# A fused attention and expert kernel: factor loads ahead of the values' stage, quantiser levels respread, five of them in the projection

## The chip, the core and the metric

The kernel runs on one core of one Trainium2 chip. The metric is device time in microseconds (us), median of three runs. Everything is fp32; matrix products are made of float32r products of high and low parts, three for each product.

The engines by the names of the profile: PE is TensorE (PEld its weight loads), DVE VectorE, ACT ScalarE, POOL GpSimd, SP SyncE, which here issues nearly all DMAs.

## What is computed

```python
x = x + attn(cond(x, itok, cond_weights), Wq, bq, Wk, bk, Wv, bv, Wo, bo, gq, gk)
x = x + ffn(cond2(x, weight, scale_log, codebook, lora_A, lora_B), A, B, Wr, br)

# cond:  W = weights[condition]; einsum('bct,bcd->bdt', x, W)      64 x 32 tokens of 512
# attn:  q, k, v = h @ W + b; RMS norm of q and k over all 4096; 32 heads of 128;
#        softmax(q k^T / sqrt(128)) v over the 32 tokens of a batch; @ Wo + bo
# cond2: a 512 x 512 weight is quantised to a 64-entry codebook
lora_delta = lora_B @ lora_A * (LORA_ALPHA / LORA_RANK)
wg = (weight + lora_delta).reshape(O, I // GROUP, GROUP)
normalized = wg / scale
idx = jnp.searchsorted(thresholds, normalized, side='left')
quantized = cb[idx]
w = jax.lax.stop_gradient(quantized - normalized) + normalized
w_eff = (w * scale).reshape(O, I) + lora_delta
return x @ w_eff.T
# ffn:   router softmax over 8 experts, low-rank A then B, weighted sum
```

## The kernel before

The 2048 tokens are 16 tiles of 128. The kernel has four parts, one after the other on TensorE.

**Mixing** forms the conditioned tokens.

**Queries and keys**: 64 steps `s`, two for each of 32 heads. Each is a block product in Strassen form: seven products `p1` to `p7` of six matmuls of 512 columns. ScalarE copies sums out of the banks (`keep_a1`, `keep_a2`, `keep_a3`), VectorE finishes the four output blocks (`block_11`, `block_12`, `block_22`; ScalarE makes the fourth), GpSimd adds squares for the norms.

**Values**: 32 more steps, `s` = 64 to 95, numbered `u` = 0 to 31, of the same seven products with the raw weights `wv` as the moving operand. The weights come in eight quads; ScalarE makes the high parts (`split_v`), and `low_v` the low parts: on VectorE at first, on GpSimd from quad 1 on, but for `low_v(1, 1)` and `low_v(2, 1)`, which VectorE does in step `u` = 0. Each output block goes from `v_out` to `v_spill` in DRAM by a store of SyncE (`store_v`), and the next block of that kind waits for the store. Two steps in, `lora(1)` multiplies the LoRA factors `la` and `lbt`.

**Projection**: 64 head pairs, in a loop over even `b`, 16 for each of four chunks `c` of tokens. A step of the loop is `pv(b)`, `pv(b + 1)` (attention weights times values), `project_out(b - 1)`, `project_out(b)`. ScalarE writes the high part of what `pv` gives (`out_hi`), VectorE the low part (`out_lo`, line 1951), which `project_out` and the pair after next wait for. VectorE also does the softmax's `shift` and `invert`, each every second step, and the transposes of the weights; GpSimd scales and normalises them and makes the low parts of the output weights (`low_o`). In between come `low_product`, which joins the effective weights with the experts' matrices, and for each chunk the residual, the router and the experts.

The **quantiser** is VectorE's filler work. A weight half of 128x1024 is built up from 63 levels: `level(half, t)` compares with a threshold, scales by the codebook step (line 1724) and adds to the sum (line 1725). After them come `straight_through` (lines 1728, 1729) and `effective` (lines 1734, 1735). Half 0 runs in the queries' stage, half 1 in the values' stage, placed by `levels_v`: one level between `block_11(s + 1)` and `block_12(s)`, the others after `block_12(s)`. Every engine takes its instructions in the order written here, with semaphores between the engines; nothing is reordered by a scheduler.

Half 1 lives in `accr`: `qv` in columns 0 to 1023, `qf` in 1024 to 2047, `update` in 2048 to 3071. `qm`, the scratch of a level, is columns 3072 to 4095 of `qreg`, where the factors `la` and `lbt` are loaded too. `xr`, two buffers of 2048 columns, holds the residual tiles of the chunks.

Of the kernel before, what the change touches and what calls it, by code (L numbers as in the profile page):

```python
# [8 lines left out]
ALU = mybir.AluOpType  # L9
# [3 lines left out]
P = 128  # L13
B, C, D = 64, 32, 512
KI = D // P
# [16 lines left out]
RANK = 64  # L32
# [23 lines left out]
V_ORDER = (0, 4, 1, 5, 2, 6, 3, 7)  # L56
B_LOW = 4
STEPS = NCH * NP
# [26 lines left out]
def levels_v(s):  # L85

    u = s - N_QK
    if u < 5 or u >= 28:
        return {28: 1}.get(u, 0)
    return 3 if u % 2 == 0 or (u % 4 == 1 and u > 5) else 2  # L90

# [19 lines left out]
def build(nc, x_nat, x_tr, cond_w, cond_idx, codebook, wqk, wv_in, wo_in, vecs, bo, w2, scale_log,  # L111
# [4 lines left out]
    with ExitStack() as ctx:  # L116
# [111 lines left out]
        wo_raw = [qk[:, 2048:3072]] + [spare[:, 1024 * (p % 2 == 0):1024 * (p % 2 == 0) + 1024] for p in range(1, NP)]  # L228
        xr = [accr[:, k:k + 2048].rearrange("p (i n) -> p i n", i=KI) for k in (0, 2048)]
        awr_sb = small[:, 0:KI * LR].rearrange("p (i n) -> p i n", i=KI)  # L230
# [200 lines left out]
        def _(sp):  # L431
# [50 lines left out]
            for s in range(1, N_QK):  # L482
                if s % 2 == 1 and (s + 3) // 2 < H:
                    load_raw((s + 3) // 2)
                if s == N_QK - 3:
                    load_v_raw(0, 0)
                if s == N_QK - 2:
                    load_v_raw(0, 1)
                if s % 2 == 0:
                    sp.wait_ge(kept, s // 2)  # L490
                    sp.dma_start(spill[s // 2 - 1], stage).then_inc(spilled, 16)
# [4 lines left out]
            load_v_raw(1, 1)  # L496
            sp.wait_ge(w_eff_done, 1)
            for rows in (slice(0, RANK), slice(RANK, P)):
                sp.dma_start(la[rows], lora_a).then_inc(ld_lora[1], 16)
                sp.dma_start(lbt[rows], lora_bt).then_inc(ld_lora[1], 16)  # L500

# [85 lines left out]
            def load_res(c):  # L587
                if c <= 1:
                    sp.wait_ge(low_raw, 2)
                else:  # L590
                    sp.wait_ge(stored, 16 * KI * (c - 1))
                sp.dma_start(xr[c % 2], x_tr[:, :, c * CH:(c + 1) * CH]).then_inc(ld_res[c % 2], 16)
# [5 lines left out]
            for b in range(2, STEPS, 2):  # L598
                c, p = b // NP, b % NP
                if b == 2:  # L600
                    for k in (11, 12, 21, 22):
                        sp.wait_ge(v_stored[k], 16 * N_V)
                if c >= 1 and p in (10, 12):
                    store_out(c - 1, p - 10)
                    store_out(c - 1, p - 9)
                if b + 2 < STEPS:
                    load_v(b + 2)
                    load_v(b + 3)
                if b + 2 < NP:
                    load_wo(b + 2)  # L610
                    load_wo(b + 3)
                if b % 4 == 0 and b // 4 + 2 < NG:
                    load_scores(b // 4 + 2)
                if b == 2 * B_LOW:
                    sp.wait_ge(low_raw, 2)
                    load_res(0)
                    sp.dma_start(b_sb, bmat).then_inc(ld_ffn, 16)
                if c == 1 and p == 2:
                    load_res(1)
                if c >= 1 and p == 14 and c + 1 < NCH:  # L620
                    load_res(c + 1)
# [458 lines left out]
        def _(act):  # L1080
# [322 lines left out]
            for b in range(2, STEPS, 2):  # L1403
# [7 lines left out]
                if b == B_LOW:  # L1411
                    low_keep(0)
                    low_keep(1)
                if b == 12:
                    act.wait_ge(ld_ffn, 48)
                    act.activation(b_part[0], b_sb, ACT.Copy).then_inc(b_hi, 1)
# [39 lines left out]
        def _(pool):  # L1456
# [129 lines left out]
            for b in range(2, STEPS, 2):  # L1586
# [6 lines left out]
                if b % 4 == 0 and b // 4 + 1 < NG:  # L1593
                    normalise(b // 4 + 1)
                if b == 16:
                    pool.wait_ge(b_hi, 1)
                    pool.tensor_tensor(b_part[1], b_sb, b_part[0].bitcast(F32), ALU.subtract).then_inc(b_lo, 1)

        @block.vector
        def _(dve):  # L1600
            chained = [0]

            def link(ins):
                chained[0] += 1
                ins.then_inc(chain, 1)
                dve.wait_ge(chain, chained[0])
# [119 lines left out]

            def straight_through(half):
                link(dve.tensor_tensor(qf[half], qf[half], qv[half], ALU.subtract))
                link(dve.tensor_tensor(qf[half], qf[half], qv[half], ALU.add))

# [227 lines left out]
            for s in range(N_QK, N_ST):  # L1958
                u = s - N_QK
                block_22(s)  # L1960
                if s + 1 < N_ST:
                    block_11(s + 1)
                if u == 1:
                    variances()
# [21 lines left out]
                block_12(s)  # L1986
                if u == 0:
                    low_v(1, 1)
                    low_v(2, 1)
                if u == 4:  # L1990
# [5 lines left out]
                if u == 28:  # L1996
                    shift(0)
                if u == 29:
                    straight_through(1)
                    effective(1)  # L2000
                if u == 30:
# [3 lines left out]
            invert(1)  # L2005
            assert taken == NCODE - 1
            def residual(c, outputs=range(KI)):
# [41 lines left out]
            for b in range(2, STEPS, 2):  # L2049
# [26 lines left out]
                if b % 4 == 0 and b // 4 + 1 < NG:  # L2076
                    invert(b // 4 + 1)
            residual(NCH - 1)

# [89 lines left out]
```

## Time and profile before

| | us |
|---|---|
| median of 3 runs | 1458.38 |
| the three runs | 1458.02, 1458.38, 1461.37 |
| the profiled execution | 1457.52 |
| its span, first to last instruction | 1455.7 |
| TensorE busy | 1447.5 (99%) |
| VectorE busy | 1082.1 (74%) |
| GpSimd busy | 750.7 (52%) |
| ScalarE busy | 726.5 (50%) |
| mean granted TensorE clock | 0.999 of full speed |

Times in the profile are from the span's start. The values' stage is from about 681 to 1006, the projection from there to the end. A row of a timeline gives start, duration, engine, line, operation, written and read tiles, shapes and count, and in square brackets the idle time of the engine before it with what ended it.

### The profile page before, as it was taken

To read this page: it belongs to the slowest core of one execution; us is meant where nothing else is said; L and a number is where in the kernel's file an instruction comes from. 1 tells how busy PE (TensorE), PEld (TensorE's weight loads), DVE (VectorE), ACT (ScalarE), POOL (GpSimd) and SP (SyncE) were. 2 spreads that over 40 slices of the span, in tenths; PEclk is the share of its full clock that TensorE was granted. 3 is DMA by queue.
4 is the path that set the end of the run, shared out by engine and by line. 5 is a ranking of instruction groups with operands and counts; after the bars stand their busy time and mean duration, and the time that the engine had idled before them with its cause. 6 is when DMAs were issued, how large, how long until landed. Compare 5 with 4: busy or idle time off the path is not lost.

```text
span 1455.7 us, 34717 instructions
## 1 busy us (share of the span) xinstructions
PE 1447.5 (99%) x14507; PEld 1201.8 (83%) x14507; DVE 1082.1 (74%) x1507; ACT 726.5 (50%) x1331; POOL 750.7 (52%) x530
## 2 busy tenths in 40 slices
PE   9999999999999999999999999999999999999999
PEld 8788888888888888888788888889888888888887
DVE  8788868687786877874469989988567667677663
ACT  7766676766766666766333333334442222222221
POOL 7668777787777777776345555514452112112100
PEclk9999999999999999999999999999999999999999
DMA  4211011110111111111443344447563334244230
GB/s 152 66 45 45 31 38 44 45 45 23 45 45 45 31 37 45 45 44 52 132 154 128 133 135 145 138 139 260 160 214 130 100 120 132 77 141 133 74 117 30
DMA packets 106989, 135.13 MB, mean 93 GB/s; under 512 B 6224, under 2 KB 89424, under 8 KB 106320
## 3 DMA queue, kind: packets, MB, share of 16 engines
q1 hardware_dynamic: 105968, 132.49, 27.6%
q8 instruction: 114, 1.87, 0.6%
q10 hardware_dynamic: 864, 0.42, 0.1%
q14 instruction: 43, 0.35, 0.1%
HBM read 86.75 MB, written 46.14 MB: 91 GB/s over the span
## 4 chain that ended last, share of the span: by engine, by line
PE 47%; DVE 4%; issue 0%; ACT 0%; DVEq 0%
PE bank L956 24%; PE bank L732 16%; PE bank L915 4%; DVE accr L1725 2%; DVE qreg L1724 1%; PE bank L984 1%; PE bank L1002 1%; DVE qk L1771 0%; PE bank L1013 0%; PE bank L970 0%; DVE sqst L1784 0%; DVE qk L1758 0%; ACT snap L1183 0%; PE bank L1034 0%; PE bank L851 0%
## 5 line engine op out<-in xcount | busy, mean ns | idle before, releaser
L713 PE MATMUL bank<-xs_hi,wa 128*128 128x512 f32 x1792 | 563.5, 392 | 0.1
L1523 POOL TENSOR_TENSOR accr<-accr,sqst 128x512 f32<-128x512 f32 x248 | 352.3, 1431 | 149.2 <-ACT sqst L1193 109.7
L713 PEld LDWEIGHTS bank<-xs_hi,wa 128*128 128x128 f32 x1792 | 336.3, 188 | 74.1 <-DVE qk L1771 2.4
L713 PE MATMUL bank<-xs_lo,wa 128*128 128x512 f32 x896 | 348.7, 389 | 0.0
L956 PE MATMUL bank<-ot,wo_main 128*128 128x512 f32 x1344 | 316.6, 392 | 0.0
L956 PEld LDWEIGHTS bank<-ot,wo_main 128*128 128x128 f32 x1344 | 249.5, 188 | 52.6
L732 PE MATMUL bank<-wv,xs_hi 128*128 128x512 f32 (+1 forms) x1008 | 284.2, 368 | 3.6 <-DVE wv L1630 2.2
L1620 DVE TENSOR_TENSOR wa<-wraw,wa 128x256 fp32r<-128x256 f32 (+1 forms) x160 | 159.2, 996 | 96.4 <-ACT wa L1102 94.7
L1318 ACT ACTIVATE ot<-bank,vec 128x256 fp32r<-128x256 f32 x256 | 100.3, 476 | 240.0 <-PE bank L956 146.6
L732 PEld LDWEIGHTS bank<-wv,xs_hi 128*128 128x128 f32 x1008 | 182.1, 189 | 38.3 <-DVE qk L1771 3.4
L1951 DVE SCALAR_TENSOR_TENSOR ot<-bank,vec,ot 128x256 fp32r<-128x256 f32 x256 | 106.1, 476 | 135.4 <-ACT ot L1318 135.0
L713 PEld LDWEIGHTS bank<-xs_lo,wa 128*128 128x128 f32 x896 | 168.3, 188 | 33.3
L732 PE MATMUL bank<-wv,xs_lo 128*128 128x512 f32 (+1 forms) x504 | 184.7, 366 | 0.0
L1566 POOL TENSOR_TENSOR wraw<-wraw,rinv 128x1024 f32<-128x1024 f32 x16 | 30.6, 1916 | 269.4 <-DVE rinv L1933 269.4
L1193 ACT ACTIVATE sqst<-qk 128x512 f32<-128x512 f32 x165 | 103.5, 627 | 62.2 <-DVE qk L1771 39.3
L1771 DVE TENSOR_TENSOR qk<-bank,snap 128x512 f32<-128x512 f32 x96 | 66.0, 688 | 76.1 <-ACT snap L1183 35.9
L1945 DVE STREAM_TRANSPOSE weights_b<-wraw 32x256 f32<-32x256 f32 x256 | 111.3, 435 | 3.6
L732 PEld LDWEIGHTS bank<-wv,xs_lo 128*128 128x128 f32 x504 | 95.3, 189 | 15.5
L1725 DVE TENSOR_TENSOR qreg<-qreg 128x1024 f32<-128x1024 f32 x63 | 104.0, 1650 | 2.2
L1725 DVE TENSOR_TENSOR accr<-accr,qreg 128x1024 f32<-128x1024 f32 x63 | 101.5, 1611 | 2.2
L1102 ACT ACTIVATE wa<-wraw 128x256 fp32r<-128x256 f32 (+1 forms) x160 | 79.0, 494 | 3.2 <-PE bank L713 3.2
L1172 ACT ACTIVATE snap<-bank,vec 128x512 f32<-128x512 f32 x64 | 44.2, 691 | 72.5 <-PE bank L713 72.5
(222 smaller groups left out, 1734.7 us busy)
## 6 DMA issues: line engine op xcount, KB each, us to landing
values_b<-v_spill SPq DMA_DIRECT2D x60, 512.0 KB, 4.8
wraw<-in_wqk SPq DMA_DIRECT2D x32, 512.0 KB, 3.5
v_spill<-qk SPq DMA_DIRECT2D x64, 256.0 KB, 2.3
v_spill<-sqst SPq DMA_DIRECT2D x64, 256.0 KB, 2.2
score_spill<-sqst SPq DMA_DIRECT2D x32, 256.0 KB, 2.0
wraw<-in_wv SPq DMA_DIRECT2D x16, 512.0 KB, 5.2
wraw<-score_spill SPq DMA_DIRECT2D x16, 512.0 KB, 4.1
spare<-in_wo SPq DMA_DIRECT2D x15, 512.0 KB, 5.7
```

Source lines behind the costliest of these rows:

```text
L713: ins = pe.matmul(dst[:, :], wa[:, col:col + P], xpart[:, j - 1, kt, n * CH:(n + 1) * CH], start=(first and k == 0), stop=(k == 5), skip_g ...
L732: ins = pe.matmul(out, xpart[:, j - 1, kt, t * P:(t + 1) * P], rhs, start=(first and k == 0), stop=(k == last), skip_group_check=True)
L956: ins = pe.matmul(bank[i][:, :], wo_slot(p)[:, wpart, col:col + P], ot[:, b % 2, opart, h, :], start=(p == 0 and k == 0), stop=(p == NP - ...
L1102: act.activation(wa[:, col:col + n], wraw[:, src:src + n], ACT.Copy).then_inc(w_hi[g], 1)
L1193: act.activation(dst, src, ACT.Square).then_inc(sq_ready, 1)
L1318: ins = act.activation(ot_part(ot[:, b % 2, 0, h, :], r), pv_part(b, r, h), ACT.Identity, bias=vec[:, 2 * (b % NP) + h, 2:3], scale=1.0)
L1523: pool.tensor_tensor(a, a, sq_slot(count), ALU.add).then_inc(acc_done, 1)
L1620: dve.tensor_tensor(wa[:, col + n:col + 2 * n], wraw[:, src:src + n], wa[:, col:col + n].bitcast(F32), ALU.subtract).then_inc(w_lo[g], 1)
L1725: link(dve.tensor_tensor(qf[half], qf[half], qm, ALU.add))
L1771: dve.tensor_tensor(dst, bank_b(s)[:, :], a3, ALU.add).then_inc(c22_done, 1)
L1945: ins = dve.transpose(pt[rows, b % 2, :, :, j * C:(j + 1) * C], src)
L1951: ins = dve.scalar_tensor_tensor(out=ot_part(ot[:, b % 2, 1, h, :], r), in0=pv_part(b, r, h), scalar=vec[:, 2 * (b % NP) + h, 2:3], in1=ot ...
```

## The change

The diff does five things. SyncE's four loads of the LoRA factors for half 1 go from behind the second raw load of the values' stage to step 62 of the queries' stage. VectorE's `low_v(1, 1)` and `low_v(2, 1)` in step `u` = 0 stand right behind `block_22` and `block_11`, not behind `block_12`. `levels_v` gives 2, 3, 3, 2 levels for `u % 4` = 0, 1, 2, 3 (it gave 3, 3, 3, 2, and 2 at `u` = 5, 1 at `u` = 28). The last five levels, `straight_through(1)` and `effective(1)` go to the projection, `b` = 2 to 14. So that this is possible `low_product` goes from `b` = 4 to 16 with what follows from it (ScalarE's copies, the load of `bmat` and its split), and the residual tiles of even chunks lie in `spare` in place of `accr`.

```diff
+LATE_LEVELS = (2, 4, 6, 8, 10)
+B_LOW = 16
-B_LOW = 4
@@ levels_v
     if u < 5 or u >= 28:
-        return {28: 1}.get(u, 0)
-    return 3 if u % 2 == 0 or (u % 4 == 1 and u > 5) else 2
+        return 0
+    return 3 if u % 4 in (1, 2) else 2
@@ build
-        xr = [accr[:, k:k + 2048].rearrange("p (i n) -> p i n", i=KI) for k in (0, 2048)]
+        xr = [t[:, 2048:4096].rearrange("p (i n) -> p i n", i=KI) for t in (spare, accr)]
@@ sync, queries' stage
                 if s == N_QK - 2:
                     load_v_raw(0, 1)
+                    sp.wait_ge(w_eff_done, 1)
+                    for rows in (slice(0, RANK), slice(RANK, P)):
+                        sp.dma_start(la[rows], lora_a).then_inc(ld_lora[1], 16)
+                        sp.dma_start(lbt[rows], lora_bt).then_inc(ld_lora[1], 16)
@@ sync, behind it
             load_v_raw(1, 1)
-            sp.wait_ge(w_eff_done, 1)
-            for rows in (slice(0, RANK), slice(RANK, P)):
-                sp.dma_start(la[rows], lora_a).then_inc(ld_lora[1], 16)
-                sp.dma_start(lbt[rows], lora_bt).then_inc(ld_lora[1], 16)
@@ load_res
-                if c <= 1:
-                    sp.wait_ge(low_raw, 2)
+                if c == 0:
+                    sp.wait_ge(pv_done, 4)
+                elif c == 1:
+                    sp.wait_ge(w_eff_done, 2)
@@ sync, projection
-                if b == 2 * B_LOW:
+                if b == 8:
+                    load_res(0)
+                if b == B_LOW:
                     sp.wait_ge(low_raw, 2)
-                    load_res(0)
                     sp.dma_start(b_sb, bmat).then_inc(ld_ffn, 16)
@@ scalar, then gpsimd: the split of bmat
-                if b == 12:
+                if b == 20:
-                if b == 16:
+                if b == 20:
@@ vector, values' stage
                 block_22(s)
+                if u == 0:
+                    low_v(1, 1)
                 if s + 1 < N_ST:
                     block_11(s + 1)
+                if u == 0:
+                    low_v(2, 1)
...
                 block_12(s)
-                if u == 0:
-                    low_v(1, 1)
-                    low_v(2, 1)
...
-                if u == 29:
-                    straight_through(1)
-                    effective(1)
@@ vector, end of the projection's loop body
+                if b in LATE_LEVELS:
+                    level(1, taken)
+                    taken += 1
+                if b == 12:
+                    straight_through(1, (0,))
+                if b == 14:
+                    straight_through(1, (1,))
+                    effective(1)
```

`straight_through` gets a second argument that picks its subtraction or its addition.

## Rows read from the trace of the kernel before

**Rows 1.** The page's first part: busy time, share of the span, instructions

```profile
PE 1447.5 (99%) x14507; PEld 1201.8 (83%) x14507; DVE 1082.1 (74%) x1507; ACT 726.5 (50%) x1331; POOL 750.7 (52%) x530
```

**Rows 2.** Timeline of TensorE around step `u` = 1: start, duration, instruction

```profile
697.21 0.28 PE L732 MATMUL bank<-wv,xs_lo 128*128 128x256 f32 x1
699.66 0.79 PE L732 MATMUL bank<-wv,xs_hi 128*128 128x512 f32 x1 [2.17 <-DVE wv L1630]
```

**Rows 3.** Windows: length, busy PE, PEld, DVE, ACT, POOL, clock, DMA share, GB/s

```profile
699.66:702.51 2.85, 2.85 (x6) 1.81 (x6) 1.63 (x1) 0.00 (x0) 2.76 (x2) 0.50 0.68 238
702.51:703.00 0.49, 0.49 (x37) 0.49 (x40) 0.00 (x0) 0.38 (x1) 0.00 (x0) 0.50 0.00 0
```

**Rows 4.** Timeline of all engines, end of step `u` = 8

```profile
784.17 0.60 ACT L1183 ACTIVATE snap<-bank 128x512 f32<-128x512 f32 x1 [0.76 <-PE bank L732]
...
786.36 0.69 DVE L1771 TENSOR_TENSOR qk<-bank,snap 128x512 f32<-128x512 f32 x1
786.47 0.39 PE L732 MATMUL bank<-wv,xs_lo 128*128 128x512 f32 x1
...
787.11 0.73 PE L732 MATMUL bank<-wv,xs_hi 128*128 128x512 f32 x2 [0.25 <-DVE qk L1771]
```

**Rows 5.** Waits, 775 to 960: total us, times, longest

```profile
PE bank L732 <- DVE qk L1771: 1.3, 5, 0.3
```

**Rows 6.** Timeline of VectorE, start of step `u` = 11

```profile
804.56 0.69 DVE L1771 TENSOR_TENSOR qk<-bank,snap 128x512 f32<-128x512 f32 x1 [0.77 <-ACT snap L1183]
```

**Rows 7.** Timeline of VectorE, step `u` = 0

```profile
691.46 0.69 DVE L1771 TENSOR_TENSOR qk<-bank,snap 128x512 f32<-128x512 f32 x1 [0.69 <-ACT snap L1183]
697.70 0.69 DVE L1758 TENSOR_TENSOR qk<-bank,snap 128x512 f32<-128x512 f32 x1 [5.55 <-DMA v_spill<-qk]
...
698.91 2.38 DVE L1630 TENSOR_TENSOR wv<-wraw,wv 128x512 fp32r<-128x512 f32 x2
```

**Rows 8.** Timelines of ScalarE and of GpSimd, the same stretch

```profile
691.24 0.63 ACT L1133 ACTIVATE wv<-wraw 128x512 fp32r<-128x512 f32 x1
...
693.91 1.30 POOL L1499 TENSOR_TENSOR qreg<-wraw 128x512 f32<-128x512 f32 x1 [4.88 <-DMA wraw<-in_wv]
```

**Rows 9.** Timeline of SyncE: time of issue, length of the issuing

```profile
670.21 0.33 SPq L491 DMA_DIRECT2D score_spill<-sqst  x1
...
689.97 0.48 SPq L499 DMA_DIRECT2D qreg<-in_lora_a  x1
...
692.41 6.37 SPq L512 DMA_DIRECT2D v_spill<-qk  x3
```

**Rows 10.** Groups by line and form: busy us, mean ns, idle us before

```profile
L1725 DVE TENSOR_TENSOR accr<-accr,qreg 128x1024 f32<-128x1024 f32 x63 | 101.5, 1611 | 2.2
...
L1724 DVE TENSOR_SCALAR qreg<-accr,thr,step 128x1024 f32<-128x1024 f32 x63 | 60.6, 962 | 0.6
...
L1729 DVE TENSOR_TENSOR accr<-accr 128x1024 f32<-128x1024 f32 x1 | 1.2, 1226 | 0.0
```

**Rows 11.** Timeline of VectorE in the projection, `b` = 10, 12 and 16

```profile
1064.88 1.66 DVE L1951 SCALAR_TENSOR_TENSOR ot<-bank,vec,ot 128x256 fp32r<-128x256 f32 x4 [3.33 <-ACT ot L1318]
...
1074.33 3.19 DVE L1925 TENSOR_TENSOR wraw<-wraw,mx 128x1024 f32<-128x1024 f32 x1
1079.38 1.66 DVE L1951 SCALAR_TENSOR_TENSOR ot<-bank,vec,ot 128x256 fp32r<-128x256 f32 x4 [1.85 <-ACT ot L1318]
...
1104.28 1.66 DVE L1951 SCALAR_TENSOR_TENSOR ot<-bank,vec,ot 128x256 fp32r<-128x256 f32 x4 [2.46 <-ACT ot L1318]
```

**Rows 12.** Timeline of GpSimd in the projection

```profile
1074.05 2.39 POOL L1579 TENSOR_TENSOR wo_main<-spare,wo_main 128x1024 fp32r<-128x1024 f32 x1 [4.96 <-ACT wo_main L1308]
```

**Rows 13.** Chain of work that ended last, projection: start, us, line, count

```profile
1027.42 3.71 PE bank L970 x32
...
1075.98 2.02 PE bank L915 x128
1078.00 11.11 PE bank L956 x48
```

More of the change, by code:

```diff
@@ L1725, in level, with straight_through @@
                 link(dve.tensor_tensor(qf[half], qf[half], qm, ALU.add))
-            def straight_through(half):
-                link(dve.tensor_tensor(qf[half], qf[half], qv[half], ALU.subtract))
-                link(dve.tensor_tensor(qf[half], qf[half], qv[half], ALU.add))
+            def straight_through(half, steps=(0, 1)):
+                for step in steps:
+                    link(dve.tensor_tensor(qf[half], qf[half], qv[half], (ALU.subtract, ALU.add)[step]))
             def effective(half):
@@ L2005, in _ @@
             invert(1)
-            assert taken == NCODE - 1
             def residual(c, outputs=range(KI)):
@@ L2077, in _ @@
                     invert(b // 4 + 1)
+                if b in LATE_LEVELS:
[6 more added lines that the diff above has]
+                    effective(1)
+            assert taken == NCODE - 1
             residual(NCH - 1)
```

## The prediction

> **What bounds the kernel now.** I read the page's first part first: TensorE is busy 1447.5 us of a span of 1455.7 [rows 1]. No other engine is above 74%, so the time is TensorE's instruction stream and whatever holes are in it. "Busy" hides holes (a matmul's end is modelled), so the second view is TensorE's timeline, where I compare starts: a 128x512 product step starts every 0.227 us (48 of them take 11.11 us in the chain of waits [rows 13], with the seam at their start), a 128x256 step every 0.12 us. Any larger distance is a hole. Outside the start-up, the end, the fixed seams of about 0.1 us after short matmuls and one of 0.19 us there are only two kinds, both in the stage of the values.
>
> First hole, once, at step 1 of that stage. The last 128x256 matmul starts at 697.21, the next one is due at 697.33 and starts at 699.66, released by VectorE's line 1630, which is `low_v(1, 1)` [rows 2]. That is 2.33 us. Then six matmuls take 2.85 us instead of 6 x 0.227 + 0.09 = 1.45: the granted clock is 0.50 (1.2 GHz) in that stretch and in the next 0.49 us [rows 3]. The engine had stood idle before the clock fell. This costs 2.85 - 1.45 = 1.40 us, and half of the 0.49 us, 0.25. Together 2.33 + 1.40 + 0.25 = 3.98 us.
>
> Second hole, five times, 38.6 us apart, the first at 787.1: `p3` waits for `block_22` behind VectorE's levels [rows 4, 5]. At 786.47 a matmul starts, the next is due at 786.70 and starts at 787.11: 0.41 us. Five of them make 2.06 us.
>
> **The change, part by part.** *`low_v(1, 1)` and `low_v(2, 1)` moved up at step 0.* Now VectorE does `block_22` at 691.46, then sits in `block_11(65)` for 5.55 us, until 697.70, because `v_out[11]` is still being stored; `block_12` and `low_v(1, 1)` are queued behind that wait and start after it, `low_v(1, 1)` at 698.91 [rows 7]. After: `low_v(1, 1)` follows `block_22`, so from about 692.15. Its input (ScalarE's split, 691.24 + 0.63) is there [rows 8]. One such operation took 1.19 us on average of the two at 698.91 [rows 7]; GpSimd's additions start only at 693.91 [rows 8]. So it is done by 694 and TensorE is due at 697.33: the hole goes whole, with 3 us to spare. Next late: `p2(66)` needs `low_v(2, 1)`. That one now stands behind `block_11(65)`. Were the store no faster, it would start at 698.3 and, at up to 1.8 us, end by 700.1. TensorE needs it after the norm sums (about 2.0 us from 698.7) and `p7` (1.44 us), at about 702.2. So 2 us of cover remain. `block_12(64)`, now behind it, is asked for only by `p5(66)`, about 4 us later still. Gain 3.98 us. I bound it below by 2.33 (were the half clock to come anyway), and above by 3.98, as no other hole lies there that this would fill.
>
> *Factor loads moved ahead.* Four DMA issues, the first at 689.97, leave the place between the raw load and the first `v_spill` store; SyncE issues that store at 692.41 and could at 689.97, 2.4 us sooner [rows 9]. They now stand at step 62 of the first stage, behind the raw load and ahead of spill 31, which SyncE issues at 670.21 [rows 9]. The raw load before them goes out at about 667.7, so they end at about 670.4 and spill 31 is late by 0.2 to 1 us; `keep_scores(31)`, which waits for it, comes 17 us later. The added wait on `w_eff_done` is for `effective(0)` of step 61, over 10 us past by then. Cost nothing; gain: the store lands up to 2.4 us sooner. With `low_v(1, 1)` moved that is cover, not time, so I add 0.
>
> *Levels respread.* A level is two instructions of 1024 columns; in this stage they average 0.96 and 1.61 us, 2.57 together [rows 10]. From step 8 on four steps held 3, 3, 3, 2 levels and now hold 2, 3, 3, 2; step 5 gets one more, step 28 loses its one, five go out. At each `u % 4 == 0`, where the hole is, one level goes. There VectorE comes to `block_22(9)` at 786.36, without idle time before it, while `a3` was ready at 784.17 + 0.60 = 784.77 [rows 4]: 1.6 us behind. Taking away 2.57 us or more puts `block_22(9)` at about 784.85, before the time from which it holds TensorE (786.36 - 0.41 = 785.95). Steps 9 and 10 keep three levels each and now begin 1.5 us earlier; before, they recovered to 0.77 us of idle time by 804.56 though they began late [rows 6]. Step 5 has some 2 us idle behind it, with 1.1 us of cover more, and takes one level. So the five holes go: 2.06 us; bounds 0 (the hole moves on to step 9) and 2.06.
>
> *Five levels and the closing steps in the projection.* VectorE has room: two head pairs take TensorE 13.13 us (11.11 + 2.02 [rows 13]), VectorE is busy 9 to 10.8 of it. What counts is `out_lo`, which gives TensorE its operand. At `b` = 10 VectorE ends its shift at 1074.33 + 3.19 = 1077.52 and starts the next `out_lo` at 1079.38 [rows 11]; an unhindered level is 0.80 + 1.22 = 2.0 us, so that `out_lo` begins 0.2 us late and ends at 1081.2. TensorE asks for it at 1078.00 + 5.55 = 1083.55 [rows 13]: 2.3 us of cover. At `b` = 8 there are 3.33 us idle [rows 11]. `b` = 14 gets the last three operations of 1.23 us [rows 10], 3.7 us, against 2.46 us of idle time [rows 11], so the next `out_lo` ends 1.3 us later than its 1105.9; `project_out(15)` lasts until 1109.9. Cost 0. A hindered VectorE instruction is seen too: 3.19 us for one that takes 1.22 alone, until GpSimd's operation of 2.39 us had ended [rows 11, 12]. If both instructions of a level meet one each, it takes 2.0 + 2 x 2.4 = 6.8 us. At `b` = 8 that gives 1061.5 + 6.8 + 1.7 = 1070.0 (3.33 us before 1064.88, one level, one `out_lo`), against the need at 1070.4: still just hidden. For five levels I take 0, with 3 us as the upper end of the cost.
>
> The Trainium skill ("SBUF — State Buffer", section "SBUF: two separate sides") says that VectorE and GpSimd hold a shared pair of ports exclusively for a whole instruction; by that rule the levels in the projection meet GpSimd's longest operations, which speaks against this part, and the price would be the 6.8 us per level above. The trace's 3.19 us row agrees with it.
>
> *Low product, loads, small edits.* `low_product` is the same 3.71 us of TensorE [rows 13], at `b` = 16 instead of 4. It asks for the effective weights, ready at about 1105.5 where TensorE arrives at 1109.9: 4.4 us of cover. Its result is needed by `pv(18)`, 5.5 us later, over 0.8 us of ScalarE's copies. The residual tile 0 goes to `spare`, whose last readers are `pv(2)` and `pv(3)`, over 40 us before. SyncE now waits for `low_raw` at `b` = 16, with the `bmat` load and the value loads of `b` = 18 behind it; these wait for `pv(18)` anyway, which comes after the low product. All 0.
>
> **The sum.** 3.98 + 2.06 = 6.0 us. The profiled execution took 1457.52 us, 0.86 below the median of 1458.38: 1451.5 by its own time, 1452.4 against the median. I give 1452.4.
>
> **Rivals.** (a) *The respread moves the hole.* Step 9 or 10, with three levels each, becomes the late one; only the first hole goes: 1458.4 - 4.0 = 1454.4. For it: GpSimd's operations last into step 9. Against: those steps recover even from a late start. (b) *Something else is next late at step 1*, or the clock falls all the same: 1452.4 + 1.65 = 1454.1, up to 1456.3 if nothing of the first hole goes. For it: many short waits meet there. Against: 2 us of cover at the next one. (c) *The projection gives a part back*, 1 to 3 us, 1453.4 to 1455.4: hindered levels at `b` = 2, 4 and 8. (d) *Slower*: the same place, but holes over 2 us. A hole of 2.33 us cost 3.98 with its half clock. It decides once a level ends more than 7.2 us after the shift or sum before it; three such holes make 12 us, 1452.4 + 12 = 1464.4. Against: even the worst level reckoned is 6.8 us. (e) *No effect*: SyncE's loads are hidden and VectorE is no bound; 1458.4. Against: both holes are released by VectorE itself.
>
> **Chances.** Forecast 0.70; (a) 0.09; (b) 0.06; (c) 0.09; (d) 0.03; (e) 0.03. About 0.3%, 4.4 us, is what a measurement of this kernel can tell from no change, so 1454.0 is the border of faster: the forecast and a little of (c) lie beyond it, 0.71. Within: 0.26. Slower: 0.03. Range: runs of one kernel differ by 3 us (1458.02 to 1461.37), which puts about 1.5 us on either side of 1452.4; above it must take in (a), (c) and most of (b). 1450.6 to 1456.4.
>
> **What would show it.** In the profile after: TensorE's six matmuls near 697.4 at 0.227 us with the clock at 1.00; `low_v(1, 1)` right after `block_22`; no row of `p3` waiting for `block_22` in the stage of the values; in the projection steps of 13.13 us without a wait for `out_lo`, though some levels stretched to 3 us and more. TensorE busy about equal to the span less 4. A TensorE wait released by line 1951 would prove (c) or (d) right; holes at a new `u % 4`, (a).

## The result and the profile after

The changed kernel takes 1450.58 us (median of 4 runs, 1450.27 to 1450.74); the kernel before, run beside it, 1459.30 us (4 runs, 1458.02 to 1461.37). The ratio is 0.9939, with a 95% interval of 0.9921 to 0.9956: 8.7 us faster. Forecast were 6.0 us and 1452.4. The time lies 0.02 us below the low end of the range, 1450.6, and the gain is 2.7 us more than forecast.

The two profiled executions differ by 7.25 us (1457.52 and 1450.27; spans 1455.7 and 1448.4). To see where, I set the starts of TensorE's matmuls against each other, one by one in the order of the program (all but the 32 of the low product, which moved), and took the difference at the borders of the stages:

| stretch | before less after, us | forecast |
|---|---|---|
| from the start to the stage of the values | 0.57 | 0 |
| first hole, step `u` = 1 | 3.91 | 3.98 |
| five holes, 38.6 us apart | 0.55 + 0.55 + 0.55 + 0.59 + 0.59 = 2.8 | 5 x 0.41 = 2.06 |
| projection | 0.0 | 0 |
| sum | 7.3 | 6.0 |

A first matmul that is late by x us is called here a hole with an idle time of x us; what the hole costs is this plus what the matmuls behind it take longer.

The page of the kernel after, its first part (busy time, share of the span, instructions):

```profile
PE 1443.8 (100%) x14507; PEld 1200.6 (83%) x14507; DVE 1079.1 (75%) x1507; ACT 726.7 (50%) x1331; POOL 746.3 (52%) x530
```

Against [rows 1], TensorE's busy time is 3.7 us shorter, though it does the same 14507 matmuls: half-clock stretches and modelled ends count as busy, and they went. The number to compare is the span.

TensorE's timeline where the first hole stood (start, duration, line, tile, count):

```profile
696.64 0.28 PE L736 MATMUL bank<-wv,xs_lo 128*128 128x256 f32 x1
696.76 0.63 PE L736 MATMUL bank<-wv,xs_hi 128*128 128x512 f32 x2
697.23 0.39 PE L736 MATMUL bank<-wv,xs_lo 128*128 128x512 f32 x1
```

The window over the same stretch (length, busy time of PE, PEld, DVE, ACT, POOL, then clock, DMA share, GB/s):

```profile
697.30:700.00 2.70, 2.70 (x141) 1.72 (x139) 0.00 (x0) 0.86 (x2) 2.70 (x3) 1.00 0.20 71
```

The last 128x256 matmul starts at 696.64, the first of 512 columns 0.12 us later. In [rows 2] that distance was 2.45 us. The clock is 1.00 where it was 0.50 [rows 3].

VectorE at step `u` = 0:

```profile
690.89 0.69 DVE L1775 TENSOR_TENSOR qk<-bank,snap 128x512 f32<-128x512 f32 x1 [0.69 <-ACT snap L1187]
691.50 0.68 DVE L1634 TENSOR_TENSOR wv<-wraw,wv 128x512 fp32r<-128x512 f32 x1
693.93 0.69 DVE L1762 TENSOR_TENSOR qk<-bank,snap 128x512 f32<-128x512 f32 x1 [1.75 <-DMA v_spill<-qk]
```

SyncE's issues, the last moved load, spill 31 and the store of `v_out[11]`:

```profile
670.85 0.60 SPq L493 DMA_DIRECT2D qreg<-in_lora_bt  x1
671.49 0.58 SPq L496 DMA_DIRECT2D score_spill<-sqst  x1
...
689.64 2.34 SPq L513 DMA_DIRECT2D v_spill<-qk  x2
```

`low_v(1, 1)` (line 1634) follows `block_22` (line 1775) at once and is done at 692.2, 4.6 us before TensorE is due. It takes 0.68 us. In the kernel before it took no longer, but came late; the chain of work that ended last has 0.62 us of it, up to 699.61:

```profile
698.99 0.62 DVE wv L1630
```

So of the 2.38 us for two such operations in [rows 7] the second, `low_v(2, 1)`, had most, 1.76. The store of `v_out[11]` is issued at 689.64 instead of 692.41 [rows 9], so VectorE waits 1.75 us for it instead of 5.55, and `block_11(65)` starts 3.04 us behind `block_22(64)` instead of 6.24. Spill 31 goes out at 671.49, 1.3 us later than in [rows 9]; TensorE waits for nothing there.

The waits of the stage of the values, 775 to 960 us (total, times, longest):

```profile
DVE qk L1775 <- ACT snap L1187: 22.1, 14, 2.6
```

This is VectorE's row: it waits for its inputs 22.1 us in all, where it was 11.6 before. TensorE has no row at all there, where [rows 5] had five waits for `block_22`. In the projection VectorE now has no idle time ahead of `out_lo` (line 1955) at `b` = 8, because its level stretched from 2.0 to 4.8 us:

```profile
1050.46 2.00 DVE L1728 TENSOR_SCALAR qreg<-accr,thr,step 128x1024 f32<-128x1024 f32 x1
1052.49 2.82 DVE L1729 TENSOR_TENSOR accr<-accr,qreg 128x1024 f32<-128x1024 f32 x1
1055.35 1.66 DVE L1955 SCALAR_TENSOR_TENSOR ot<-bank,vec,ot 128x256 fp32r<-128x256 f32 x4
```

TensorE's only wait of any size that is left in the whole run is one of 1.0 us for a GpSimd result near the start, which the kernel before has too.

### The profile page after: what moved, and what is told of

Its sections match the earlier page's. It is cut to its first block, busy times and chain, and to the rows that moved or that the text cites. A ratio compares the mean times of both kernels' runs of the same rounds, so it can differ in the third digit from the quotient of the medians.

```text
span 1448.4 us, 34721 instructions
## 1 busy us (share of the span) xinstructions
PE 1443.8 (100%) x14507; PEld 1200.6 (83%) x14507; DVE 1079.1 (75%) x1507; ACT 726.7 (50%) x1331; POOL 746.3 (52%) x530
## 4 chain that ended last, share of the span: by engine, by line
PE 97%; DVE 1%; ACT 1%; DMA 0%; issue 0%; SPq 0%; DVEq 0%
PE bank L717 42%; PE bank L960 25%; PE bank L736 21%; PE bank L919 4%; PE bank L845 3%; PE bank L988 1%; PE bank L1006 1%; DMA qk<-in_x_nat 0%; PE bank L666 0%; DVE qreg L1708 0%; PE bank L1017 0%; PE bank L974 0%; ACT xs_hi L1160 0%; DVE wa L1624 0%; DVE sqst L1708 0%
## 5 line engine op out<-in xcount | busy, mean ns | idle before, releaser
L1197 ACT ACTIVATE sqst<-qk 128x512 f32<-128x512 f32 x165 | 103.7, 628 | 61.3 <-DVE qk L1775 38.6
```

What stands on the lines that cost most here:

```text
L1197: act.activation(dst, src, ACT.Square).then_inc(sq_ready, 1)
```

## The experiments

Times are medians. Ratios are against the kernel before, run on the same chip within the same comparison (its medians: 1459.09 for the first four kernels, 1459.43 for the next eight, 1457.87 for the last four). "Cost of the first hole" is the difference in TensorE's starts from just ahead of it to some 70 us behind it, against the profile of the kernel after.

**Neither part: the kernel before again.**

> The kernel before, unchanged, with the span and clock of every run. The forecast fell short by 1.3 us in the profiled executions (7.3 against 6.0) and by more in the medians (8.7). Theory 1: the first hole (2.33 us of idle TensorE, then half clock) costs not the same in every run, since the time at half clock varies; then this kernel's runs spread over 2 us or more and the slow ones show the lower mean clock. Theory 2 (rival): the before runs scatter from something else, and span and clock do not go together. The ratio itself must be 1.000.

Measured: 1458.88 (11 runs, 1456.68 to 1463.16), ratio 1.0005 [0.9994, 1.0016]. The same program ranges over 6.5 us. In this execution the first hole cost 5.67 us, not 3.91:

```profile
700.50 0.73 PE L732 MATMUL bank<-wv,xs_hi 128*128 128x512 f32 x2 [2.47 <-DVE wv L1630]
...
702.00:708.80 6.80, 6.80 (x150) 4.97 (x150) 0.13 (x1) 0.76 (x2) 1.27 (x1) 0.50 0.08 26
708.80:711.00 2.20, 2.20 (x15) 1.95 (x14) 1.50 (x4) 0.95 (x2) 1.17 (x1) 0.99 0.02 8
```

The engine stands idle 0.3 us longer than in [rows 2], as the store that `block_11(65)` waits for lands that much later. The half clock lasts 6.8 us instead of 3.34, and it begins only at 702.0, when TensorE has been at work again for 1.5 us. The later holes are as they were, 0.55 to 0.59 us each.

**The changed kernel again.**

> The changed kernel, unaltered, beside the four below on one chip. By the experiments so far the two moves at step 0 give about 4 us and the levels 2 us in the median, 6 together, while the changed kernel was 8.7 us faster. If the parts only add up, this one is 6 us faster, near 1453. If they need each other (a moved low_v leaves a fifth hole of 1.8 us that only the respread closes; the respread alone leaves the first hole), 8 us or more, 1450.5, all clocks 1.000, spread under 1 us.

Measured: 1451.33 (5 runs, 1450.17 to 1451.66), 0.9941 [0.9929, 0.9952]. Its runs lie within 1.5 us and all have a mean clock of 1.000.

**`low_v` alone, loads alone, both.** The first kernel is the one before with only those hunks of the change that move the two `low_v` of step 0; the second moves only the four factor loads; the third does both. All three leave the levels as they were.

> Only the two low_v of VectorE moved up. Theory 1: the first hole goes whole with its half clock, 3.9 us in the profile and more in the median, clock 1.000 in all runs, spread under 1 us. The five holes behind the levels stay, at 0.55 us each by the trace after (0.42 and 0.11 on the step behind it), not the 0.41 of the forecast. Rival: a part of it needs the earlier factor loads too; then under 3 us.

> Only the four factor loads moved. The forecast put 0 on this part alone beside the moved low_v. Alone, the store lands 3.8 us sooner (693.9 by the trace after), block_12 then runs when p3 is done and low_v(1, 1) ends near 696 to 697, TensorE being due at 697.3: this part alone would close the first hole as well, 3 to 4 us faster. Rival: low_v(1, 1) meets GpSimd's additions and comes 1 us late; then a hole under 1 us and no half clock, 2.5 to 3.5 us faster.

> low_v moved and factor loads moved, levels as before. Either of them alone closed the first hole, so the second adds nothing: 3.7 to 4 us faster, as each alone. Rival: the loads add cover that shows in the spread or a further us.

Measured: 1455.10 (10 runs), 0.9975 [0.9965, 0.9984]; 1455.44 (8 runs), 0.9972 [0.9959, 0.9985]; 1454.78 (6 runs), 0.9967 [0.9955, 0.9978]. The first hole is gone in each: its cost is 0.0, and the mean clock is 1.000 in all runs. So each of the two moves closes it alone, and the second adds nothing that these runs can tell. With the loads alone VectorE still does `low_v(1, 1)` behind `block_12`, but the store is issued 2 us sooner and the whole row moves up:

```profile
694.85 0.69 DVE L1758 TENSOR_TENSOR qk<-bank,snap 128x512 f32<-128x512 f32 x1 [2.37 <-DMA v_spill<-qk]
695.46 0.68 DVE L1784 TENSOR_TENSOR sqst<-bank,snap 128x512 f32<-128x512 f32 x1
696.06 3.03 DVE L1630 TENSOR_TENSOR wv<-wraw,wv 128x512 fp32r<-128x512 f32 x2
```

Here the first of the two `low_v` ends at 697.39 and TensorE starts at 697.66: 0.3 us to spare, where the moved `low_v` has 4.6.

In all three the cost of the fifth of the later holes grew from 0.59 to 1.95 or 2.0 us. VectorE's rows of the first of the three there:

```profile
931.99 2.29 DVE L1725 TENSOR_TENSOR accr<-accr,qreg 128x1024 f32<-128x1024 f32 x1
934.32 1.67 DVE L1724 TENSOR_SCALAR qreg<-accr,thr,step 128x1024 f32<-128x1024 f32 x1
936.02 2.34 DVE L1725 TENSOR_TENSOR accr<-accr,qreg 128x1024 f32<-128x1024 f32 x1
938.40 0.69 DVE L1771 TENSOR_TENSOR qk<-bank,snap 128x512 f32<-128x512 f32 x1
```

GpSimd's in the same stretch:

```profile
931.91 3.52 POOL L1554 TENSOR_TENSOR wv<-qreg,wv 128x512 fp32r<-128x512 f32 x2 [3.21 <-ACT wv L1133]
935.99 1.29 POOL L1554 TENSOR_TENSOR wv<-wraw,wv 128x512 fp32r<-128x512 f32 x1 [0.56 <-ACT wv L1133]
```

Two instructions of line 1725 start just after one of GpSimd's (931.99 after 931.91, 936.02 after 935.99) and take 2.3 us instead of 1.23. In the profile of the kernel before, the pair that corresponds to the first came the other way round, line 1725 at 935.72 (1.23 us) and GpSimd at 935.84; the second took 2.20 us there too, so nearly all of the growth is the first. I read from this that an offset of a tenth of a microsecond decides over more than a microsecond; no run set the offset on purpose. By the profiles 3.9 us gained early left some 2.5 at the end of the stage.

**The levels and the projection alone.**

> Only the levels: respread, five and the closing steps in the projection with all that goes with it; factor loads and low_v as before. By the trace after five holes of 0.55 us go, 2.8 us faster, ratio 0.998, with the first hole still there, clock below 1.000 and the spread of the kernel before. By the forecast's price, 2.1 us. Rival: the projection gains or loses something of its own.

Measured: 1457.07 (12 runs, 1453.94 to 1459.24), 0.9987 [0.9977, 0.9997]. The five holes are gone (0.0 each) and the projection costs nothing; the first hole is there and cost 6.75 us in the profiled execution: an idle time of 3.72 us, then the half clock from about 703.3 to 710. It is longer than in the kernel before because `block_11(65)` waits 0.3 us longer and `low_v(1, 1)` takes 1.8 us beside GpSimd instead of 0.7, the program being the same up to there:

```profile
698.81 0.69 DVE L1762 TENSOR_TENSOR qk<-bank,snap 128x512 f32<-128x512 f32 x1 [5.86 <-DMA v_spill<-qk]
699.42 0.68 DVE L1788 TENSOR_TENSOR sqst<-bank,snap 128x512 f32<-128x512 f32 x1
700.01 3.48 DVE L1634 TENSOR_TENSOR wv<-wraw,wv 128x512 fp32r<-128x512 f32 x2
```

Single runs with a mean clock of 1.000 took 1453.9 to 1454.3, those at 0.998 1456.6 to 1458.4. By medians the parts don't add up: 4.7 us for both moves at step 0 and 2.0 us for this part, against 8.1 us for the whole. The 1.4 us that are missing are as much as the fifth hole grows when step 0 alone is changed, which the respread closes; that the first hole of this part cost more than in the profile of before may add to it.

**`low_v` back in its old place in the changed kernel.**

> The changed kernel with both low_v of step 0 back behind block_12. As the loads alone closed the first hole, this is within 0.5 us of the changed kernel. Rival: low_v(1, 1) now meets GpSimd's additions and ends after 696.8; then a hole of 0.3 to 1 us without half clock.

Measured: 1451.67 (5 runs, 1451.60 to 1451.72), 0.9944 [0.9932, 0.9956]; no hole. The loads carry it, with 0.4 us to spare in the profile: `low_v(1, 1)` ends at 697.88 and TensorE starts at 698.23.

**Number or place of the levels.** Two kernels change only the function that spreads them. The first puts all 63 levels in the stage, two at each `u % 4 == 0` and three elsewhere, and leaves step 0 as before. The second is the changed kernel, with its own number of levels but three at `u % 4 == 0`:

```diff
-    return 3 if u % 4 in (1, 2) else 2
+    return 3 if u % 4 in (0, 1) or u == 6 else 2
```

> Only levels_v altered: 2 levels where u % 4 is 0, 3 everywhere else (2 at u = 7), all 63 in the values' stage, closing steps there too, nothing in the projection. It tells whether the five holes go because of where the levels stand or because five of them left. By the forecast's reading (hole at u % 4 = 0 alone) the five holes go and it is as fast as the levels part alone, 2 us; rival: with 11 levels in four steps a hole turns up at u % 4 = 3 or 0, where GpSimd adds and VectorE waits for it; then 0 to 1 us, or slower.

> The changed kernel with the same number of levels in the values' stage, but placed 3, 3, 2, 2 by u % 4 instead of 2, 3, 3, 2: the step u % 4 == 0 has three again, as before the change. Theory 'place' (the hole at the start of u % 4 == 1 is made by the third level ahead of block_22 of that step, and GpSimd's operations beside it): holes come back once every four steps, 0.55 us each and one of some 2 us as in the kernels with the old levels, together 2.8 to 4.2 us over the changed kernel: 1453.5 to 1455. Theory 'count' (the stage merely had some levels too many): no hole, the time of the changed kernel, within 1 us of 1451.

Measured, the first: 1466.15 (6 runs), 1.0045 [1.0032, 1.0057], slower than the kernel before: the reading that the holes go with the step `u % 4 == 0` alone was wrong here, and what its rival said came, only dearer. The first hole cost 6.7 us; four more came where `block_22` of `u` = 12, 16, 20 and 24 is due, at the end of three steps with three levels each, one of 2.75 us with a half clock behind it (4.5 us in all) and three that cost 1.6 to 1.8 us at full clock. Its waits:

```profile
PE bank L732 <- DVE qk L1771: 6.6, 4, 2.6
PE bank L732 <- DVE wv L1630: 3.6, 1, 3.6
```

Measured, the second: 1453.25 (4 runs), 0.9952 [0.9936, 0.9969]. All five holes are back at their old place, 0.55 us each, 2.77 us in the profile:

```profile
PE bank L736 <- DVE qk L1775: 1.3, 5, 0.3
```

The number of levels is that of the changed kernel, so the place makes the hole.

**All 63 levels in the stage, in better places.** Both moves at step 0, levels 2, 3, 4, 2 by `u % 4` from step 7 on and 3 up to step 6; the closing steps in the stage, nothing in the projection:

```diff
-    if u < 5 or u >= 28:
-        return {28: 1}.get(u, 0)
-    return 3 if u % 2 == 0 or (u % 4 == 1 and u > 5) else 2
+    if u < 5 or u >= 28:
+        return 0
+    return 3 if u < 7 else (2, 3, 4, 2)[u % 4]
```

> The kernel before with both moves at step 0, and all 63 levels and the closing steps in the values' stage as before, nothing of them in the projection; only the spread over the steps differs: 2, 3, 4, 2 by u % 4 from step 7 on and 3 up to step 6. Theory 'place alone is enough' (five levels need not go to the projection once the step u % 4 == 0 is relieved and the step u % 4 == 2, which had idle time, takes four): no hole, 1450.5 to 1452. Theory 'the stage is too full' (a fourth level of 2.57 us does not fit a step's idle time): holes at the start of u % 4 == 3 of 0.5 to 2.6 us, five of them, 1453.5 to 1464, the upper end with a half clock behind each.

Measured: 1451.59 (4 runs, 1450.37 to 1454.27, that longest one at a mean clock of 0.999), 0.9944 [0.9924, 0.9963]; in the profiled execution the places of the five holes cost 0.02 to 0.03 us each. After four levels VectorE comes to `block_22` 0.44 us before its input:

```profile
809.65 0.69 DVE L1771 TENSOR_TENSOR qk<-bank,snap 128x512 f32<-128x512 f32 x1 [0.44 <-ACT snap L1183]
```

By the median this equals the changed kernel, within what can be told here. Its longest run is an open end: no run of the changed kernel (nine) was as long or had a mean clock below 1.000, and no profile shows what happened in this one. So carrying five levels to the projection was not needed for the median: giving the crowded step one less and the idle one four does the same.

**How much room the projection has.** The changed kernel with two more instructions of a level's kind at each even `b` up to 14 (the results are not used), and with four more:

```diff
+                if b <= 14:
+                    link(dve.tensor_scalar(qm, qv[1], thr[:, 1:2], step[:, 0:1], ALU.is_gt, ALU.mult))
+                    link(dve.tensor_tensor(qm, qm, qv[1], ALU.add))
```

> The changed kernel with one more level's worth of VectorE instructions (two of 1024 columns, result not used) at every even b up to 14, where two more made TensorE wait six times, 23 us in all, and cost 37 us. Theory 'cover of one hindered level': at b = 8 and 10 the second level brings out_lo 0 to 2 us after TensorE's need, at b = 0, 12 and 14 it is hidden; 0 to 6 us lost, 1451.5 to 1457. Theory 'room for it' (unhindered it is 2.0 us and 2.3 to 4.0 us of cover are there): nothing lost, within 1 us of 1451.3. Theory 'ports' (each added instruction meets one of GpSimd's and grows to 2.8 us or more): 10 us or more lost.

> The changed kernel with four more VectorE instructions of a level's size at every even b up to 14 of the projection (their results are not used): two more levels' worth, 4.0 us unhindered, at b = 0 to 14. Theory 'cover' (the projection is free because out_lo has 2.3 to 4 us of cover): at b = 8, with its level already 2.8 + 2.0 us, another 4 us or more bring out_lo 0 to 3 us after TensorE asks for it, the same at b = 2, 4, 6 and 10, less at 12 and 14; TensorE waits there for lines 1951 and 1955, 1 to 3 us in each of four or five places, and 4 to 15 us are lost, more where the clock falls to half behind a hole: 1455 to 1470. Theory 'VectorE has slack without limit here' (a late out_lo is made good by the score product in between): within 1 us of the changed kernel.

Measured: with two, 1466.93 (4 runs), 1.0067 [1.0050, 1.0084]; with four, 1489.84 (4 runs), 1.0207 [1.0186, 1.0228]. In the profiles they cost 14.5 and 37.0 us, more than I expected from cover alone. The first has four waits of TensorE for `out_lo`, three of 8.6 us in all and one of 1.4 at the low product; before the longest, at `b` = 4, VectorE does this:

```profile
1026.44 0.71 DVE L1728 TENSOR_SCALAR qreg<-accr,thr,step 128x1024 f32<-128x1024 f32 x1
1027.19 2.82 DVE L1729 TENSOR_TENSOR accr<-accr,qreg 128x1024 f32<-128x1024 f32 x1
1030.05 2.78 DVE L2083 TENSOR_SCALAR qreg<-accr,thr,step 128x1024 f32<-128x1024 f32 x1
1032.86 3.27 DVE L2084 TENSOR_TENSOR qreg<-qreg,accr 128x1024 f32<-128x1024 f32 x1
1036.16 1.66 DVE L1955 SCALAR_TENSOR_TENSOR ot<-bank,vec,ot 128x256 fp32r<-128x256 f32 x4
```

GpSimd beside it:

```profile
1026.60 2.33 POOL L1570 TENSOR_TENSOR wraw<-wraw,rinv 128x1024 f32<-128x1024 f32 x1 [1.12 <-DVE rinv L1937]
1028.89 3.39 POOL L1565 TENSOR_TENSOR wraw<-wraw,rqk 128x1024 f32<-128x1024 f32 x1
1032.24 2.81 POOL L1583 TENSOR_TENSOR wo_main<-spare,wo_main 128x1024 fp32r<-128x1024 f32 x1
```

Two levels side by side with GpSimd take 9.7 us (1026.44 to 1036.13) instead of 4.0; the second of them takes 6.1. The two alternate: VectorE's instructions end at 1030.01, 1032.83 and 1036.13, which is 1.1, 0.6 and 1.1 us after GpSimd's end at 1028.93, 1032.28 and 1035.05, and GpSimd's ends come 2.2 to 2.3 us after VectorE's. Each of these stretches is about the time of one such instruction by itself (0.80 or 1.22 us on VectorE, 2.39 on GpSimd in [rows 12]) or less. The Trainium skill ("SBUF — State Buffer", section "SBUF: two separate sides") calls the shared ports an exclusive lock held for the whole instruction; the trace agrees with that rule. So of the three theories that of the ports fits, with its 10 us or more, and the two others fall.

**A hole of chosen length.** The changed kernel with `low_v(1, 1)` and `low_v(2, 1)` back behind `block_12`, and one to four copies of 512 columns ahead of them (the copies write a tile that is not in use):

```diff
+                if u == 0:
+                    for _ in range(1):
+                        link(dve.tensor_copy(rqk[:, :], ones[:, 0:1].broadcast_to([P, 512])))
+                    low_v(1, 1)
+                    low_v(2, 1)
```

> The changed kernel with low_v(1, 1) and low_v(2, 1) back behind block_12 of step 0 and four VectorE copies of 512 columns ahead of them: a hole before TensorE's products of the first low value, of chosen length, with nothing else of the change undone. By VectorE's rows low_v(1, 1) stood ready about 1.2 us ahead of TensorE's need without the copies; four copies of about 0.4 to 0.55 us take 1.6 to 2.2 us, so the hole should be 0.5 to 1.5 us. Theory 'a short hole costs itself' : clock 1.00 throughout and 0.5 to 1.7 us over the changed kernel. Theory 'any hole here drops the clock': a further 1.7 us (3.3 us at 1.2 GHz) or 3.4 us (6.7 us at 1.2 GHz).

> As the kernel with four copies ahead of low_v(1, 1) (there the copies took 1.33 us each, the hole was 5.2 us, and 9.3 us were lost), with one copy: low_v(1, 1) comes 4.0 us sooner, so the hole is about 1.2 us. Theory 'price by length' (a hole up to 2.0 us was never followed by a half clock here, at 2.3 us and over always): clock 1.00 in all runs, loss equal to the hole, 1.2 to 1.4 us: about 1452.7. Theory 'any hole drops the clock': 1.7 to 3.4 us more, 1454.4 to 1456.

> The same with two copies: the hole is about 2.6 us. Theory 'price by length with a jump': in some runs the clock stays at 1.00 and 2.6 to 2.8 us are lost (1454), in others it falls to half for 3.3 or 6.7 us and 1.7 or 3.4 us come on top (1455.5 to 1457.5): single runs spread over some 3 us, as those of the kernel before. Theory 'fixed price': all runs within 1 us.

> The same with three copies: the hole is about 3.9 us. Theory 'price by length with a jump': a half clock in every run, most of 6.7 us: 3.9 + 3.4 = 7.3 us lost, about 1458.5, and no run at a mean clock of 1.000. Theory 'fixed price': 3.9 + 1.7 = 5.6 us, 1457.

The first of these texts is that of the kernel with four copies. Its copies took 5.32 us, not 2, so its hole was far longer than meant. GpSimd was at work beside them, to which I put it down; no run has such a copy by itself. Measured in the profiled execution, and over all runs:

| copies | idle beyond the normal distance, us | cost in that profile, us | clock behind it | median of the runs, us | their mean clocks |
|---|---|---|---|---|---|
| 0 (`low_v` back alone) | 0 | 0.0 | 1.00 | 1451.67 (1451.60 to 1451.72) | 1.000 in all |
| 1 | 1.17 | 1.29 | 1.00 | 1452.13 (1451.97 to 1452.24) | 1.000 in all |
| 2 | 2.60 | 2.71 | 1.00 | 1454.30 (1453.07 to 1456.19) | 1.000 in five, 0.999 in three, 0.998 in one |
| 3 | 4.05 | 7.07 | 0.50 for some 7 us | 1457.46 (1455.59 to 1458.69) | 0.999 to 0.996, none at 1.000 |
| 4 | 5.37 | 9.31 | 0.50 for some 9 us | 1457.79 (1456.59 to 1460.08) | 0.999 to 0.996, none at 1.000 |

The windows behind the hole with two copies:

```profile
702.00:704.00 2.00, 2.00 (x138) 1.23 (x136) 0.35 (x1) 0.60 (x1) 1.49 (x1) 1.00 0.00 0
704.00:706.00 2.00, 2.00 (x18) 1.64 (x14) 0.00 (x0) 0.00 (x0) 0.00 (x0) 1.00 0.04 8
```

With three copies:

```profile
704.00:705.00 1.00, 1.00 (x65) 0.84 (x67) 0.00 (x0) 0.60 (x1) 0.00 (x0) 0.50 0.00 0
...
709.00:710.00 1.00, 1.00 (x6) 1.00 (x6) 0.00 (x0) 0.00 (x0) 0.00 (x0) 0.50 0.00 0
```

An idle time of 2.60 us cost only 0.11 us more than itself here; one of 2.33 us cost 3.91 us in the profile before [rows 2, 3], one of 2.63 us cost 5.67 when the kernel before ran again. Three more are in the profiles above: two of 2.27 us in the projection of the kernel with four more instructions, which cost 4.0 us each, and one of 2.75 us of the kernel with 63 levels, 4.5 us, all with a half clock behind. The windows behind the first of these, where TensorE starts at 1061.66:

```profile
1059.00:1062.00 3.00, 0.89 (x5) 0.45 (x4) 2.95 (x7) 2.35 (x5) 0.00 (x0) 1.00 0.59 186
1062.00:1064.00 2.00, 2.00 (x7) 1.58 (x6) 1.93 (x5) 0.17 (x1) 1.76 (x1) 0.55 0.00 0
```

So between about 2.3 and 2.8 us the length alone does not decide; by their mean clocks the runs of one program show both. Below (up to 1.83 us) no half clock followed in any profile, and with one copy in no run; above (3.7 us and more) one followed in every profile, and with three or four copies in every run. The Trainium skill ("TensorE: Matmul & The Clock Gate", section "Part 1: The HAM clock gate") says of the start of a kernel that the number of matmuls at the low clock differs from run to run; these runs show a difference from run to run in the middle of one, too.

## Why the prediction was right or wrong

*The first hole*: right in mechanism and in size for the profile that it was read from (3.98 forecast, 3.91 found). It closed as forecast, `low_v(1, 1)` right after `block_22`, the clock at 1.00. The step that failed is the one that leads from there to the median. I took the cost of the hole in one execution, 3.98 us, for its cost in all, and read the 3 us between the runs as noise on both kernels alike. Much of it was the hole. It cost 3.91, 5.67, 6.75 and 6.73 us in four profiled executions of kernels that keep it, and two things differ between them: the idle time, 2.33, 2.63, 3.72 and 3.73 us, by when the store lands and by whether `low_v(1, 1)` takes 0.7 us or, beside GpSimd, nearly 1.8; and the half clock, 3.3 us in the first and 6.8 in the others. Without the hole the runs of a kernel lie within 0.1 to 2.2 us (3.9 in the kernel with all levels in the stage) instead of 6.5. The kernel before shows it run by run. In the last comparison, nine of its 18 runs had a mean clock of 1.000 and took 1455.6 to 1458.4 us, the other nine 0.999 to 0.996 and 1457.4 to 1462.4. The profile at hand was one of the cheaper ones (1457.52 against a median of 1459.30 in the same comparison, 1.8 us); that of the kernel after lies only 0.3 us under its median (1450.27 against 1450.58). The medians differ by 8.7 us and the profiles by 7.25, so this makes up 1.5 of the 2.7 us that the forecast lacked. That the median's share is this hole is read from clocks and spread; no profile was taken of those runs. The time came out 1.8 us under the forecast, so the 1.5 us on either side that the prediction takes from the spread of three runs do not hold it; they give a low end of 1450.9, not the 1450.6 that it states.

*The loads*: I booked them as cover worth no time, since `low_v` would have moved as well. True of the pair, but either alone would have done: the loads alone, and `low_v` alone, bring the cost of the hole to 0.0. The size was off: I had the store up to 2.4 us sooner, and `block_11(65)` starts 3.2 us sooner after `block_22(64)`. As the loads alone leave 0.3 us to spare, 2.4 us would by this reckoning have left a hole of 0.5. The 0.2 to 1 us for spill 31 were 1.3, with no effect.

*The five holes*: right in cause and place; the size was off, 2.06 us forecast, 2.8 found. The term counted only the missing distance ahead of the first late matmul, 0.41 us. The start behind it is late too: in [rows 4] the pair at 787.11 lasts 0.73 us instead of the 0.62 or 0.63 of an undisturbed pair, another 0.11 us each time, and 0.03 us more follow. The same 0.11 us stand behind the holes made on purpose (1.17 us idle cost 1.29, 2.60 cost 2.71). 5 x 0.14 = 0.7 us.

*Start to values*: 0.57 us of the profiled difference fall ahead of any changed step but the loads. Against the profile of the kernel after, other executions of it were there at -0.1 and, with `low_v` put back, at +1.5 us. I take it for the scatter of that stretch; no run ties it to an edit.

*The respread*: right that the crowded step is `u % 4 == 0`, and right against rival (a): steps 9 and 10 held. The runs show more than I had claimed. With as many levels in the stage as in the changed kernel the holes come back when the places are the old ones.

*The projection*: the forecast cost of 0 held, with the hindered levels it named (4.8 us for one; 6.8 was the worst reckoned). Rivals (c) and (d) did not come about, but the runs with more levels show how near they were. At `b` = 8 `out_lo` ended at 1057.0 against a need at about 1059.4, 2.4 us of cover, and one more level can cost 6.1 us, as the second did at `b` = 4 of the kernel with one more. With one put in at every even `b` to 14, it cost 14.5 us in the profile, some 11 of them idle time (starts later than due by 4.6, 3.7, 0.8 and 1.7 us) and most of the rest half clock. A chance of 0.03 for (d) was fair for this change; the upper end of 3 us for five levels was not a limit of the mechanism, only of the cover that this placement happens to leave.

*Low product, residual tile, SyncE's new wait*: 0, as forecast; the projection's difference is 0.01 us with all of them in it. They were not tried one by one.

*Rival (b)*, something else late at step 1, and *(e)*, no effect: neither came. (The upper figure of (b) is 1456.4 by its own sum, not 1456.3.)

The sign, the places and the cover were right. The number missed for two terms of the sum, 0.7 us of restarts and some 1.5 us because the first hole has no one price; the 0.6 us ahead of the stage are the rest of the 2.7.

What stays open is what decides in a given run whether the clock falls behind an idle time of 2.3 to 2.8 us, and for how long. No run here set it on purpose.

## What to carry to other kernels

If a kernel's runs spread more than its neighbours' do, look for one idle time of 2 to 4 us on TensorE: its cost can differ from run to run, which one profile doesn't show. Here closing it moved the median by more than the profile at hand said, which was a cheap one; the next may be a dear one. Where VectorE's filler work makes TensorE wait, try to place it anew before moving it to another stage: here one level less in the crowded step and four in the idle one gave the median that the move gave. A step that is given more filler can become the late one, as the kernel with three levels nearly everywhere shows. Price VectorE work of this kind that can meet GpSimd's at up to three times its time alone (the second level above took 6.1 us instead of 2.0), and count the cover that is left after that.

## What the runs showed of the hardware

A level's two instructions take 0.80 and 1.22 us alone and 2.78 and 3.27 us beside GpSimd's of 128x1024 in the rows above; a copy of 512 columns took 1.33 us on average beside GpSimd's of 1.3 to 1.5 us. One that started 0.12 us ahead of GpSimd's took 1.23 us and one that started 0.08 us behind took 2.29, and in three kernels a gain of 3.9 us upstream went with 1.4 us lost at a hole downstream.

The clock need not fall while TensorE is idle: behind idle times of 2.63, 3.72 and 4.05 us it started at full clock, and the granted clock fell to 0.50 between 1.0 and 1.5 us later, when it was at work again; behind the one of 2.33 us it fell as TensorE started.

Where TensorE starts again at full clock after a hole, of 0.41 to 4.05 us, the pair of matmuls that ends it takes 0.11 us longer (0.73 instead of 0.62).
